# A fused attention and mixture-of-experts block on one core: the front rewritten (x in both layouts, logits as columns of a product, row scales from Ln and Exp), and 12 of 16 w_lo pieces on GpSimd

## The reference, cut to what matters

```python
qkv = x @ W_qkv + b_qkv                       # x: 16 batches of 256 tokens of 128
q, k, v = split(qkv)
attn = softmax(q @ k.T / sqrt(128))
x = layernorm(x + (attn @ v) @ W_out + b_out)              # x1
h = x + layer_norm(x, ln1_g, ln1_b) @ attn_w.T
t = layer_norm(h, ln2_g, ln2_b)
logits = t @ gate_w.T                                       # 8 experts
top_vals, top_idx = top_k(logits, 2); rw = softmax(top_vals)
for e in range(8):
    out += comb[:, e] * (silu(t @ gate_proj[e].T) * (t @ up_proj[e].T)) @ down_proj[e].T
out = layernorm(x1 + h + out)     # the residual is x1 plus (h plus the experts)
```

## Time and profile before

| | |
|---|---|
| median of 3 runs | 405.9 us (404.86 to 407.33) |
| profiled execution, first to last instruction | 403.7 us |
| DVE busy | 287.6 us, 71% of the span |
| PE busy | 309.9 us, 77% |
| POOL busy | 210.4 us, 52% |
| ACT busy | 189.6 us, 47% |

### The profile page before, as it was taken

The page is one execution under the profiler, slowest core; times in us unless marked ns, Lnnn a source line. Parts: engine busy times, 40 slices in busy tenths (PEclk is TensorE's granted clock), DMA queues, the critical chain, the costliest instruction groups (busy, mean ns, idle before and its releaser), DMA issues.

```text
span 403.7 us, 9351 instructions
## 1 busy us (share of the span) xinstructions
PE 309.9 (77%) x2041; PEld 268.2 (66%) x2042; DVE 287.6 (71%) x1108; ACT 189.6 (47%) x474; POOL 210.4 (52%) x276
## 2 busy tenths in 40 slices
PE   3999888888765204999999999999999999970000
PEld 2788777776544103888888898988888898860000
DVE  2589999999998725766666666666666666634992
ACT  3887757677643202444444434344443434420552
POOL 0031888788787785243434343444434444354992
PEclk9999999999975555999999999999999999995555
DMA  6610111144511131112111111111111111105871
GB/s 200 198 52 26 42 63 57 54 145 151 198 35 41 47 94 25 41 39 56 42 52 39 52 41 45 50 40 52 39 52 41 45 50 39 42 12 156 213 205 53
DMA packets 33853, 29.52 MB, mean 73 GB/s; under 512 B 4753, under 2 KB 31381, under 8 KB 33696
## 3 DMA queue, kind: packets, MB, share of 16 engines
q1 hardware_dynamic: 24576, 18.36, 16.3%
q0 software_dynamic: 4320, 8.47, 6.1%
q10 hardware_dynamic: 4928, 2.36, 2.0%
HBM read 18.02 MB, written 11.61 MB: 73 GB/s over the span
## 4 chain that ended last, share of the span: by engine, by line
PE 54%; DVE 29%; issue 7%; DMA 4%; POOL 3%; ACT 2%; SPq 0%; DVEq 0%; ACTq 0%; POOLq 0%
PE bank L503 15%; PE bank L465 8%; PE bank L467 8%; PE bank L466 8%; PE bank L493 8%; DVE y L715 2%; DVE rows L673 2%; PE bank L476 2%; DVE x_all L873 2%; POOL expert_rows L913 2%; DVE n L658 2%; DVE st L754 1%; DVE st L721 1%; DVE topi L780 1%; DVE w_lo L769 1%
## 5 line engine op out<-in xcount | busy, mean ns | idle before, releaser
L963 POOL DMA_INDIRECT moe_rows<-ysb,idx x71 | 71.3, 1005 | 35.6 <-issue 18.5
L503 PE MATMUL bank<-wd,hidT 128*128 x568 | 75.4, 276 | 0.7 <-ACT ysb L608 0.6
L913 POOL DMA_INDIRECT expert_rows<-rows,place x64 | 63.4, 990 | 17.9 <-issue 13.9
L859 DVE SCALAR_TENSOR_TENSOR hid<-sg,xrow,bank 128x512 f32<-128x512 f32 x71 | 53.1, 748 | 24.2 <-PE bank L467 22.5
L503 PEld LDWEIGHTS bank<-wd,hidT 128*128 128x128 f32 x568 | 69.0, 192 | 1.4 <-issue 1.3
L608 ACT ACTIVATE ysb<-bank 128x128 f32<-128x128 f32 x71 | 19.8, 278 | 102.6 <-PE bank L503 102.6
L465 PE MATMUL bank<-w_hi,t_hi 128*128 x142 | 62.2, 438 | 3.8 <-DVE t_lo L851 3.8
L959 POOL TENSOR_TENSOR idx<-xrow,zero_i 128x1 int32<-128x1 int32 x71 | 12.7, 180 | 86.9 <-issue 56.9
L849 DVE CAST t_hi<-t 128x128 fp32r<-128x128 f32 x71 | 19.9, 281 | 51.8 <-ACT t L595 51.8
L467 PE MATMUL bank<-w_hi,t_lo 128*128 x142 | 56.5, 398 | 0.0
L466 PE MATMUL bank<-w_lo,t_hi 128*128 x142 | 56.2, 396 | 0.0
(11 more groups left out here) (122 smaller groups left out, 592.7 us busy)
## 6 DMA issues: line engine op xcount, KB each, us to landing
xrow<-expert_rows SPq DMA_DIRECT2D x71, 65.0 KB, 1.8
w_raw<-weights SPq DMA_DIRECT2D x16, 256.0 KB, 3.9
yin<-moe_rows SPq DMA_DIRECT2D x16, 256.0 KB, 3.8
xin<-x SPq DMA_DIRECT2D x16, 128.0 KB, 2.2
wd<-weights SPq DMA_DIRECT2D x1, 2048.0 KB, 9.2
out<-x_all ACTq DMA_DIRECT2D x16, 128.0 KB, 3.3
moe_rows<-ysb,idx POOLq DMA_INDIRECT x71, 2.4
expert_rows<-rows,place POOLq DMA_INDIRECT x64, 2.3
```

What stands on the lines that cost most here:

```text
L503: last = mm(banks[7][:, 0:P], hidT[i2][:, c * P:(c + 1) * P], wd[:, bass.ds(w + c * P, P)], start=(c == 0), stop=(c == NC - 1))
L859: V.scalar_tensor_tensor(hid[i2][:, :], sg[i2][:, :], xrow[r1][:, D:D + 1], banks[2 + i2][:, :], ALU.mult, ALU.mult).then_inc(sm["hid_done ...
L913: G.indirect_dma_start(out=expert_rows[:, :], out_offset=bass.IndirectOffsetOnAxis(ap=place[b % NR][:, t, k:k + 1], axis=0), in_=rows[b % ...
L963: G.indirect_dma_start(out=moe_rows[:, :], out_offset=bass.IndirectOffsetOnAxis(ap=idx[r3][:, :], axis=0), in_=ysb[r3][:, :], in_offset=No ...
```

## The change

The host passes x twice, once as before and once transposed (`xt`), so PE's transposes of x and ACT's copies of them go. The products of a norm are reordered: `attn_w` and `gate_w` are first multiplied by the norm's gain and cleared of their mean (`wa`, 144 columns, made once in a longer start), PE transposes x1 itself (L455) and one product (L477) gives the 128 columns of attn_w and two times 8 columns for the logits, and DVE applies the row scale after it (L873, L792 to L809). So the normed y and normed h are no longer made, nor is the transpose of the latter. The bias of v enters as a product (L407), and the sum of the probabilities as a 129th column of L507. The raw h goes to the experts with its mean and scale beside it, and DVE norms it there (`tn`, one more pipeline step). From the first norm on, batches go in groups: batch 0, then seven pairs, then batch 15. In a group's odd step the first norm (`g_v`) and the routing (`g_r`) are worked on, in its even step x1's transposes, `nT` and h (`g_n`). The pipeline has 21 steps in place of 22.

The scales of the norms come from ACT now: Ln, then Exp with scale -0.5 (L622, L624 for the first norm, L659, L661 for the second), and DVE improves the seed in three small instructions. POOL has no pow left in the front. It begins with 12 of the 16 `w_lo` subtractions and then sends the rows; a DMA on SP's queue makes the second copy of each row. The addition of h to x1 is cut in 64 pieces of 64 columns that POOL does in the experts loop.

```diff
+GROUPS = [[0]] + [[b, b + 1] for b in range(1, B - 1, 2)] + [[B - 1]]
+GROUP_OF = {b: g for g, bs in enumerate(GROUPS) for b in bs}
+ENDS_AT = {bs[-1]: g for g, bs in enumerate(GROUPS)}
...
-        PIECES = [3, 3, 2, 3, 0, 0, 0, 0, 0, 0, 0, 0, 0, 0, 1, 0, 1, 1, 1, 1, 0, 0]
+        PIECES = [3, 3, 3, 3, 0, 0, 0, 1, 0, 1, 0, 1, 0, 1]
+        BY_POOL = 12
...
-        FRONT = 6
+        FRONT = 5
...
+                        j = i - NWR
+                        sp.wait_ge(sm["wlo_pool"], j + 1) if j < BY_POOL else sp.wait_ge(sm["wlo_done"], j + 1 - BY_POOL)
...
+                g = ENDS_AT.get(s - 4)
+                if g is not None:
+                    sp.wait_ge(sm["mv2_done"], tiles(g).stop)
+                    if g >= 2:
+                        sp.wait_ge(dup_in[g % 2], turn(g - 2, g % 2, 2))
+                    sp.dma_start(rows[:, tiles(g), 1, 0:D + 1], rows[:, tiles(g), 0, 0:D + 1]).then_inc(dup_in[g % 2], 16)
+                if s == B:
+                    sp.dma_start(wd[:, :], w_v[:, 2, :]).then_inc(sm["wd_in"], 16)
...
+                if g_n is not None:
+                    if g_n >= 1:
+                        pe.wait_ge(sm["n1T_sb"], g_n)
+                    else:
+                        pe.wait_ge(sm["wa_ready"], 1)
+                    for j in range(count(g_n)):
+                        pe.wait_ge(sm["x1_done"], tiles(g_n).start + j + 1)
+                        last = nc.tensor.transpose(ps_n[:, tok(j)], xs_tile(tiles(g_n).start + j), ident)
+                    last.then_inc(sm["n1T_ps"], 1)
...
+                if g_n is not None:
+                    for b in GROUPS[g_n]:
+                        pe.wait_ge(sm["n1T_sb"], g_n + 1)
+                        if b >= 2:
+                            pe.wait_ge(sm["h_done"], NT * (b - 1))
+                            pe.wait_ge(sm["zb_done"], GROUP_OF[b - 2] + 1)
+                        else:
+                            pe.wait_ge(sm["wa_ready"], 1)
+                        for t in range(NT):
+                            j = NT * b + t - tiles(g_n).start
+                            last = mm(ps_a[side(b)][:, t, :], nT[g_n % 2][:, tok(j)], wa[:, :], start=True, stop=True)
+                        last.then_inc(sm["a_ps"], 1)
+                if live(0) and s >= 1:
+                    qk(s)
+                    values(s)
...
+                if g_r is not None:
+                    m, n = member[g_r % 2], count(g_r)
+                    pe.wait_ge(sm["member_done"], g_r + 1)
...
-                            last = mm(ps_o[:, tok(t)], probT[b % 2][:, kt, tok(t)],
-                                      vo[b % 3][:, kt, :], start=(kt == 0), stop=(kt == NT - 1))
+                            last = mm(ps_o[:, t, :], probT[b % 2][:, kt, tok(t)],
+                                      vo[b % NV][:, kt, 0:D + 1], start=(kt == 0), stop=(kt == NT - 1))
...
+            def query_key(b):
+                act.wait_ge(sm["k_ps"], b + 1)
+                if b >= 2:
+                    act.wait_ge(sm["s_ps"], b - 1)
+                A(qT[b % 2][:, :], ps_q, ACT.Identity, bias=bq_s[:, :], scale=QSCALE).then_inc(sm["q_sb"], 1)
+                A(kT[b % 2][:, :], ps_k, ACT.Identity, bias=col(BK)).then_inc(sm["q_sb"], 1)
+
+            def values(b):
+                act.wait_ge(sm["v_ps"], b + 1)
+                if b >= NV:
+                    act.wait_ge(sm["o_ps"], b - NV + 1)
+                else:
+                    act.wait_ge(sm["vo_ones"], NV)
+                A(vo[b % NV][:, :, 0:D], ps_v, ACT.Copy).then_inc(sm["v_sb"], 1)
...
+                if g_v is not None:
+                    g, n = g_v, count(g_v)
+                    act.wait_ge(sm["v0_done"], 2 * g + 2)
+                    if g >= 2:
+                        act.wait_ge(sm["r0_done"], g - 1)
+                    A(ln0[g % 2][:, :, 0:n], v0[g % 2][:, :, 0:n], ACT.Ln).then_inc(sm["ln0_done"], 1)
+                    act.wait_ge(sm["ln0_done"], g + 1)
+                    A(seed0[g % 2][:, :, 0:n], ln0[g % 2][:, :, 0:n], ACT.Exp, scale=-0.5).then_inc(sm["seed0_done"], 1)
+                if live(0) and s >= 1:
+                    query_key(s)
+                    values(s)
+                if g_v is not None:
+                    g = g_v
+                    act.wait_ge(sm["shift0_done"], g + 1)
+                    act.wait_ge(sm["y_done"], tiles(g).stop)
+                    act.wait_ge(sm["r0_done"], g + 1)
+                    for j in range(count(g)):
+                        at = xs_tile(tiles(g).start + j)
+                        A(at, at, ACT.Identity, bias=shift0[g % 2][:, j:j + 1], scale=r0[g % 2][:, 0, j:j + 1]
+                          ).then_inc(sm["x1_done"], 1)
...
                         A(prob[b % 2][:, t, :], ps_s[:, t * S:(t + 1) * S], ACT.Exp,
-                          bias=negmax[b % 2][:, t:t + 1], accum_out=rsum[b % 3][:, t:t + 1]
-                          ).then_inc(sm["prob_done"], 1)
+                          bias=negmax[b % 2][:, t:t + 1]).then_inc(sm["prob_done"], 1)
+                for i in pieces(s):
+                    act.wait_ge(w_in[i % NWR], turn(i, i % NWR, NWR))
+                    A(w_hi[:, :, i * WP:(i + 1) * WP], w_raw[i % NWR][:, :, :], ACT.Copy).then_inc(sm["whi_done"], 1)
+                if g_n is not None:
+                    g, n = g_n, count(g_n)
+                    act.wait_ge(sm["v2_done"], g + 1)
+                    if g >= 2:
+                        act.wait_ge(sm["r2_done"], g - 1)
+                    A(ln2[g % 2][:, 0:n], v2[g % 2][:, 0:n], ACT.Ln).then_inc(sm["ln2_done"], 1)
+                    act.wait_ge(sm["ln2_done"], g + 1)
+                    A(seed2[g % 2][:, 0:n], ln2[g % 2][:, 0:n], ACT.Exp, scale=-0.5).then_inc(sm["seed2_done"], 1)
...
-                        V.scalar_tensor_tensor(y[b % 2][:, t, :], ps_o[:, t * P:(t + 1) * P], rinv[b % 2][:, t:t + 1],
-                                               xin[b % NX][:, t, :], ALU.mult, ALU.add).then_inc(sm["y_done"], 1)
-                if live(3):
-                    b = s - 3
+                        V.scalar_tensor_tensor(xs[:, b, t, :], ps_o[:, t, 0:D], rinv[b % 2][:, t:t + 1],
+                                               xs[:, b, t, :], ALU.mult, ALU.add).then_inc(sm["y_done"], 1)
...
+                if g_r is not None:
+                    g, n = g_r, count(g_r)
+                    dve.wait_ge(sm["seed2_done"], g + 1)
+                    V.scalar_tensor_tensor(half2[:, 0:n], v2[g % 2][:, 0:n], -0.5, seed2[g % 2][:, 0:n],
+                                           ALU.mult, ALU.mult).then_inc(sm["half2_done"], 1)
+                    dve.wait_ge(sm["a_ps"], GROUPS[g][-1] + 1)
+                    i2 = ratio[g % 2][:, 0:n].rearrange("p (b t) -> p b t", t=NT)
+                    as4 = lambda a: a[:, 0:n, :].rearrange("p (b t) e -> p b t e", t=NT)
+                    wide = [P, n // NT, NT, E]
+                    V.tensor_tensor(as4(za), ps_logits(g, D + E), i2.unsqueeze(3).to_broadcast(wide), ALU.mult
+                                    ).then_inc(sm["za_done"], 1)
+                    dve.wait_ge(sm["half2_done"], g + 1)
...
+                    V.tensor_tensor(as4(zb), ps_logits(g, D), as4(za), ALU.add).then_inc(sm["zb_done"], 1)
...
+                    dve.wait_ge(sm["seed0_done"], g + 1)
+                    V.scalar_tensor_tensor(half0[:, :, 0:n], v0[g % 2][:, :, 0:n], -0.5, seed0[g % 2][:, :, 0:n],
+                                           ALU.mult, ALU.mult).then_inc(sm["half0_done"], 1)
+                    dve.wait_ge(sm["half0_done"], g + 1)
+                    V.tensor_tensor(corr0[:, :, 0:n], half0[:, :, 0:n], seed0[g % 2][:, :, 0:n], ALU.mult
+                                    ).then_inc(sm["corr0_done"], 1)
+                    dve.wait_ge(sm["corr0_done"], g + 1)
+                    if g >= 2:
+                        dve.wait_ge(sm["x1_done"], tiles(g - 2).stop)
+                    V.scalar_tensor_tensor(r0[g % 2][:, :, 0:n], corr0[:, :, 0:n], 1.5, seed0[g % 2][:, :, 0:n],
+                                           ALU.add, ALU.mult).then_inc(sm["r0_done"], 1)
+                    dve.wait_ge(sm["r0_done"], g + 1)
+                    V.tensor_tensor(sd0[:, :, 0:n], v0[g % 2][:, :, 0:n], r0[g % 2][:, :, 0:n], ALU.mult
+                                    ).then_inc(sm["sd0_done"], 1)
...
+                            k = NT * b + t
+                            V.scalar_tensor_tensor(rows[:, k, 0, 0:D], ps_a[side(b)][:, t, 0:D],
+                                                   ratio[g % 2][:, k - first:k - first + 1], xs[:, b, t, :],
+                                                   ALU.mult, ALU.add).then_inc(sm["h_done"], 1)
...
+                    if i < BY_POOL:
+                        continue
                     dve.wait_ge(sm["whi_done"], i + 1)
                     cs = slice(i * WP, (i + 1) * WP)
                     V.tensor_tensor(w_lo[:, :, cs], w_raw[i % NWR][:, :, :], w_hi[:, :, cs].bitcast(F32),
```

(24 more changed lines are left out.)

886 lines of the change are left out of this document (441 added, 445 removed).

## The result

The changed kernel takes 471.1 us (median of 5 runs, 470.09 to 473.69) against 406.05 for the kernel before (5 runs, 404.86 to 407.35): 1.160 times the time, 95% interval 1.156 to 1.164. Forecast were 446 us and at most 462. The profiled execution is one of the five, 473.7 us with a span of 471.8.

A forecast was written before the change was run, and what follows sets the result against it. DVE was taken to pace the front and PE the experts; after the change, rounds through ACT's loads and waits and PE's clock. 403.7 + 43.7 (front) - 3.4 (handover and experts) + 2.2 around the span gave 446 us, range 424 to 462.

The forecast's parts named there:

- The start and the rounds: Front: step 5's rinv at 38.8 us, then rounds of two batches at 18.9 us, 9.5 a batch where it was 6.95.
- ACT was above 75% busy: Front: a sign that the prediction is right, ACT's busy share there above 75%.
- The loads: ACT in the front: four table loads a round at 1.28 us, 5.1 us in ACT's 13.3 us of work.
- The dearer price: Rival on ACT's front loads: each holds ACT up to 1.78 us, all 36 on the chain, 462 us; chance 0.06.
- Hidden loads: Rival in the front: loads fall into ACT's idle time, DVE binds, rounds of 12.8 us, 394 us in all; chance 0.13.
- The clock: PE in the front: some 6 us of nothing each round lowers its clock, so the burst behind costs 2.1 us more.
- POOL's pieces: Start: POOL's 12 subtractions of 512 columns take 1.26 us each, 15.1 in all, ahead of its first row DMA, costing nothing.
- The front's end and the handover: After the rounds: POOL's last row DMA done at 191.9 us, +43.7; handover and experts together net -3.4 us.
- The experts: Experts loop: POOL's adds and DVE's tn, 0.3 us a tile each, stay below PE's 2.87 us a tile; finish unchanged.
- a lost cover: Experts loop: if tn at 0.3 us a tile were not hidden below PE, 0.3 x 71 = 21 us.
- The clock did not hold: Rival in the front, "the clock holds": PE's burst comes at full clock, 431 us; chance 0.17.
- Faster or level: Outcomes outside the 8-in-10 range: the hidden-loads rival (faster, 0.13) and no change (404 to 408 us, 0.03).

The follow-up runs named there:

- both repairs: Changed kernel with eight index buffers in place of four and one log-and-exp table set loaded ahead: 404.5 and 405.3 us without the unplaced waits, 433.4 us with them.
- sets 1, 2 and 4: Three groups of runs, each sharing a chip, in which the unplaced waits appeared; the kernel before took 409.9, 411.9 and 407.3 us in them.
- sets 3 and 5: Two groups of runs, each sharing a chip, in which the unplaced waits were absent; the kernel before took 406.1 and 406.3 us.
- e11_ref: Changed kernel with eight index buffers and the common table set loaded ahead, a reference run without the unplaced waits: 404.5 us.

## Why the prediction was right in the front and wrong in the experts

**The start and the rounds: right, and mostly by the terms.** `rinv` of step 5 came at 36.35 us for 38.8. From it to that of step 15 (128.73) are five rounds of 18.5 us, for 18.9. In the round shown ACT's work was 13.56 us for 13.3; its waits 3.1 for nT (forecast 1.2, and 2.1 for the clock), 1.4 for qT (1.7), 0.2 and 0.2 (0.3 and 0.3). That ACT was above 75% busy was wrong, 70 to 72%, but not the sum.

**The loads: right that they stand on the chain and last 1.28 us, too dear in what they cost.** There are 38, 36 of them in the front. Taking them out shortened a round by 4.8 to 5.0 us with a part of the clock's loss in it; the loads alone stand for 3.9 of their 5.13, because other waits of ACT grow in their place. The dearer price, 1.78 us, does not hold: the next activation starts 0.01 us behind a load. Hidden loads do not hold for this kernel where its front is undisturbed; the 12.8 us that this rival gave for a round are near the 13.5 to 13.7 that a round takes without any load. The Trainium skill ("ScalarE: Activation LUTs", What ACT_TABLE_LOAD costs) would add a drain of 1.38 us for each; the activation at 93.09 starts 0.01 us behind the load that ends at 93.08, and no run here shows a drain on ACT's timeline. The Trainium skill (the same page, Table sets: the hidden batching unit) says that one set holds both exp and ln. The runs bear this out, but the built program had four loads a round until the set was named by hand.

**The clock: right as a wait, somewhat too dear, and not to be had back by idle work.** Over the five rounds the wait for nT was 2.9 us, against the 1.2 of a round at full clock: 1.7 us a round, for 2.1. Added matmuls that nobody reads brought no time back; taking the loads out brought about 1 us a round.

**POOL's pieces: right.** Twelve pieces at 1.24 to 1.26 us were done at 34.5, and the first row DMA came at 47.86, 13.4 us behind.

**The front's end and the handover: right.** The last row DMA was off POOL at 187.7 us (186.76 + 0.96) for 191.9: the start was 2.4 us and the five rounds 2.1 us shorter than forecast, what follows step 15 was 0.4 longer. From there to the first gate product 6.3 us passed, where it had been 9.4: -3.1 us for -3.4.

**The experts: wrong, and here lies the miss.** The step that failed reads "both lie below PE's 2.87 us for a tile" and "The finish stays", and ahead of it "nothing the change does to other engines in the experts stage matters while they stay below it". Both additions did lie below it, as said; the busy shares that the step argued from were right, too. But the change also had a third part there, the one more pipeline step that its description names, over rings of four, and the prediction put it at nothing without a reason. It closed a circle of 3.3 us (2.6 of a scatter in flight, 0.66 of POOL) around what had had two tiles' time before. Its price is 31.7 us in the first profile (28.6 in the stage, 3.1 behind it, where the last four scatters are issued one behind the other), 30.7 by taking it out, and 25.6 when the wait is put into the kernel before. The forecast's 446 with this term, and the front and handover as they came (3.9 under the forecast), gives 473.8, and the profiled execution took 473.7; as all these terms are read off that same profile, the sum only says that nothing else is missing, while the price itself rests on the 30.7. The price named for a lost cover, 21 us, was of the right size by chance: it was for `tn`, and with `tn` in place and the ring widened the stage takes what it took before. One of the prediction's own signs of being wrong did come, "tiles over 2.9 us apart": they are 232.3 / 71 = 3.27.

**Rivals.** None of the four had the ring. The clock did not hold (grant 0.79 in the front). Faster or level, 0.16, did not come about; both repairs together are level with the kernel before, 0.996 to 0.998. Two of the rivals' sums are off by a little: 1.78 - 1.28 is 0.50 and not 0.45, which gives 464 us for dearer loads, and the gains of the hidden loads add up to 13.1 and not 12, which gives 393. Neither changes anything above.

## What to carry to other kernels

When a loop gets a pipeline step more, count for each ring the steps between the last use of a buffer and its next filling, DMAs in flight included, before looking at busy shares: a stage with PE at 100% can be one buffer away from a bound that no engine's share shows. The timeline of the kernel before showed the two lengths that decide it, the scatter's time to land and the distance of two scatters. And where Ln and Exp alternate, name the table set that holds both, ahead of the first of them.

## What the runs showed of the hardware that was not expected

A release by PE reached DVE and ACT late, DVE mostly by 4 to 5 us (1.7 to 6.7), in five rounds of every profile of the changed front in sets 1, 2 and 4, and in none of sets 3 and 5, though set 3 and set 4 had the same chip (with different kernels on it). It costs the changed kernel 11 to 12 us, the one with both repairs 28 to 29 us, and the kernel before was 1 to 6 us slower in those sets. Moving the weight load did not remove it, nor did more work on PE; what it hangs on is open. The price of the loads without it, 36 to 38 us of front with what the clock gives back, therefore rests on a comparison between sets of runs, in which the kernel before took 406.05 and 406.1 to 406.3 us; within one set it is measured only with the waits there, 21.0 us (19.4 with the ring widened).

PE's half clock cost a round 1.3 us (14.3 against 13.0 in e11_ref) to 1.9 us (the nT wait of the changed kernel's round, 3.1 against 1.2), although the eight value matmuls are only 1 us longer: the scores behind them are slow too, and ACT's chain waits for both. In the changed kernel PE stood for 5.9 us a round ahead of `member` and the burst behind was at half clock in all five rounds; in e11_ref it stood for 2.0 and two bursts of five were.
